# One mask product for a whole group of score tiles in place of one per tile

## What is computed

```
scores = jnp.einsum('bqd,bkd->bqk', hidden, keys)
scores = jnp.where(mask[:, None, :] == 0, NEG_INF, scores)
weights = jax.nn.softmax(scores, axis=2)
context = jnp.einsum('bqk,bkd->bqd', weights, values)
```

## Time and profile before

| | |
|---|---|
| median of 3 runs | 594.95 us (594.57 to 598.1) |
| span of the profiled execution | 602.9 us |
| TensorE busy | 565.9 us, 94% of the span |
| VectorE busy | 453.7 us, 75% |
| ScalarE busy | 377.1 us, 63% |
| mean granted TensorE clock | 0.997 of 2.4 GHz |

### The profile page before, as it was taken

One profiled execution on the slowest core, in us unless ns is written; L12 is line 12 of the kernel. 1 busy time (PEld: TensorE's weight loads), 2 busy tenths in 40 slices (PEclk: granted clock), 3 DMA queues, 4 the chain that ended last, 5 costly groups with the idle time before them and its releaser, 6 DMA issues.

```text
span 602.9 us, 12930 instructions
## 1 busy us (share of the span) xinstructions
PE 565.9 (94%) x3952; PEld 466.3 (77%) x3952; DVE 453.7 (75%) x1246; ACT 377.1 (63%) x729; POOL 257.7 (43%) x291
## 2 busy tenths in 40 slices
PE   7988999998989999999999999979889899999997
PEld 6787888886769999999999988867645555655654
DVE  5987888876645877778888863668888798867755
ACT  5676778864525777777777663345664684775643
POOL 4445665554550234455444445666635551310100
PEclk9999999999989999999999999999999999999999
DMA  8334654442238778879998827462112420200000
GB/s 237 107 108 148 210 196 163 145 167 88 106 123 254 278 255 268 276 230 285 273 274 276 274 85 285 138 213 79 52 37 73 130 96 36 71 2 35 36 36 35
DMA packets 47973, 93.15 MB, mean 154 GB/s; under 512 B 6990, under 2 KB 17306, under 8 KB 47778
## 3 DMA queue, kind: packets, MB, share of 16 engines
q1 hardware_dynamic: 39740, 74.34, 37.1%
q0 software_dynamic: 7440, 17.97, 9.9%
q10 hardware_dynamic: 726, 0.02, 0.1%
HBM read 61.32 MB, written 32.17 MB: 155 GB/s over the span
## 4 chain that ended last, share of the span: by engine, by line
PE 57%; DVE 20%; ACT 7%; issue 7%; POOL 4%; DMA 2%; SPq 2%; another core or an unknown queue 1%; ACTq 0%; DVEq 0%; POOLq 0%
PE bank L1336 12%; PE bank L1334 12%; PE bank L1335 11%; PE bank L1832 5%; DVE st L2408 3%; PE bank L1853 3%; PE bank L1854 2%; POOL yr L731 2%; DVE g3l L2485 2%; DVE xa L2399 2%; DVE sl L2480 2%; PE bank L1675 2%; PE bank L1320 2%; PE bank L1301 1%; DVE xa L2463 1%
## 5 line engine op out<-in xcount | busy, mean ns | idle before, releaser
L635 POOL DMA_INDIRECT rows_by_expert<-n,pos x64 | 64.6, 1009 | 53.6 <-DVE pos L2136 37.1
L683 POOL TENSOR_TENSOR yg<-yg,b 128x512 f32<-128x512 f32 x31 | 46.8, 1509 | 93.9 <-ACT yg L823 93.9
L731 POOL DMA_INDIRECT yr<-expert_out,out_row x64 | 65.0, 1016 | 33.4 <-issue 19.1
L1832 PE MATMUL bank<-m4Th,wint 128*128 128x512 f16 x192 | 69.0, 380 | 5.5 <-DVE sl L2480 3.3
L1334 PE MATMUL bank<-xTh,wph 128*128 128x256 f32 x248 | 72.3, 291 | 0.5 <-issue 0.4
L1336 PE MATMUL bank<-xTh,wpl 128*128 128x256 f32 x248 | 70.1, 283 | 0.0
L1335 PE MATMUL bank<-xTl,wph 128*128 128x256 f32 x248 | 70.1, 282 | 0.0
L1832 PE MATMUL bank<-m4Tl,wint 128*128 128x512 f16 x192 | 68.8, 379 | 0.0
L2301 DVE TENSOR_TENSOR wpl<-wraw,wph 128x1024 fp32r<-128x1024 f32 x40 | 49.0, 1224 | 11.3 <-ACT wph L823 11.2
L823 ACT ACTIVATE wph<-wraw 128x1024 fp32r<-128x1024 f32 x40 | 42.4, 1060 | 14.1 <-PE bank L1336 9.3
L2480 DVE SCALAR_TENSOR_TENSOR sl<-bank,sl 128x512 f32<-128x512 f32 x48 | 33.0, 688 | 22.5 <-ACT sl L1137 22.4
(11 more groups left out here) (352 smaller groups left out, 1740.6 us busy)
## 6 DMA issues: line engine op xcount, KB each, us to landing
wraw<-in_wexp SPq DMA_DIRECT2D x40, 512.0 KB
xg<-rows_by_expert SPq DMA_DIRECT2D x31, 256.0 KB, 4.1
expert_out<-yg SPq DMA_DIRECT2D x31, 256.0 KB, 3.5
x_shared<-x SPq DMA_DIRECT2D x8, 512.0 KB
xa<-x_shared SPq DMA_DIRECT2D x4, 1024.0 KB
out<-ost SPq DMA_DIRECT2D x8, 512.0 KB, 2.7
xin<-in_x SPq DMA_DIRECT2D x7, 512.0 KB, 4.2
stage<-in_wexp SPq DMA_DIRECT2D x8, 256.0 KB
```

The lines of the kernel that those rows point to most:

```text
L635: pool.indirect_dma_start(out=xs, out_offset=bass.IndirectOffsetOnAxis(ap=pos[p][:, k, j:j + 1], axis=0), in_=n2[p][:, j, :], in_offset=No ...
L683: pool.tensor_tensor(yg[u % 3], yg[u % 3], b2[:, bass.ds(e, 1), :].broadcast_to([P, 2, D]), ALU.add)\
L731: pool.indirect_dma_start(out=yr[:, c, k, j, :], out_offset=None, in_=ys, in_offset=bass.IndirectOffsetOnAxis(ap=out_row[:, b * GB + c, k, ...
L1832: last = mm(bank[:, 2 * (m % 2) + w, :], wt[:, k, m * P:(m + 1) * P], part[c][:, k, :], start=(q == 0 and k == 0), stop=(q == 1 and k == K ...
```

## The change

In `scores`, the mask product is taken out of the loop over the four tiles. Behind the loop stands one product of the same `onesb` by `barred`, whose 77 columns are read four times over (a broadcast operand), and which writes the 77 columns of each of the four tiles: 308 columns in all. It gives `s_done`. In `scores_half` the same is done for two tiles, 154 columns, and the wait for `mask_ready` moves from between the first tile and its mask to behind both tiles. The flag that begins an accumulation is now set on the first product of the bank alone, and not on the first of each tile.

```diff
@@ scores(g, b)
                 for j in range(GT):
                     o = bank[:, 6, j * P:j * P + KV]
                     for k in range(KD):
-                        mm(o, n1T[:, k, j * P:(j + 1) * P], ctxC[:, k, b, :], start=(k == 0), stop=False)
-                    last = mm(o, onesb, barred[:, b, :], start=False, stop=True)
-                last.then_inc(sem("s_done"), 1)
+                        mm(o, n1T[:, k, j * P:(j + 1) * P], ctxC[:, k, b, :], start=(j == 0 and k == 0), stop=(j == 0 and k == KD - 1),
+                           skip_group_check=(j > 0))
+                every = bank[:, 6, :].rearrange("p (j n) -> p j n", j=GT)[:, :, 0:KV]
+                mm(every, onesb, barred[:, b, :].unsqueeze(1).broadcast_to([P, GT, KV]), start=False, stop=True,
+                   skip_group_check=True)\
+                    .then_inc(sem("s_done"), 1)
@@ scores_half(h)
                 for j in range(2):
                     o, t = bank[:, 6 - 4 * h, j * P:j * P + KV], 2 * h + j
                     for k in range(KD):
-                        mm(o, n1T[:, k, t * P:(t + 1) * P], ctxC[:, k, 0, :], start=(k == 0), stop=False)
-                    if h == 0 and j == 0:
-                        pe.wait_ge(sem("mask_ready"), 1)
-                    last = mm(o, onesb, barred[:, 0, :], start=False, stop=True)
-                last.then_inc(sem("s_done"), 1)
+                        mm(o, n1T[:, k, t * P:(t + 1) * P], ctxC[:, k, 0, :], start=(j == 0 and k == 0), stop=(j == 0 and k == KD - 1),
+                           skip_group_check=(j > 0))
+                if h == 0:
+                    pe.wait_ge(sem("mask_ready"), 1)
+                both = bank[:, 6 - 4 * h, 0:2 * P].rearrange("p (j n) -> p j n", j=2)[:, :, 0:KV]
+                mm(both, onesb, barred[:, 0, :].unsqueeze(1).broadcast_to([P, 2, KV]), start=False, stop=True,
+                   skip_group_check=True)\
+                    .then_inc(sem("s_done"), 1)
```

## The result

The changed kernel takes 597.43 us, the median of 20 runs (594.54 to 603.62). The kernel before, on the same chip, takes 594.87 us, also 20 runs (593.42 to 598.2). The ratio is 1.004, with a 95% interval of 1.0024 to 1.0056: **slower by 0.4%**. That lies outside the predicted range, which ended at 596.8, and it is a loss where a gain of 0.4 us was forecast. It did stay within 1%, which had the chance of 0.95.

The account below looks back on a forecast made before the run. TensorE, busy 94% of the span, was taken to bound the kernel. Per full group -3 x 0.065 + 0.095 = -0.10 us, over four groups on the chain 0.40 us, gave 594.95 - 0.40 = 594.5 us, range 593.2 to 596.8.

Parts of the forecast that it names:

- The price of a tile: Scores loop on TensorE: a tile without mask takes 0.448 us in place of 0.513, so a removed product is worth 0.065.
- The wide product: Behind the four tiles of scores: 308 columns cost 0.13 us, 0.095 more than the narrow product.
- Rival 3: Scores: broadcast operand and four-piece target make the wide product dear, 595.4 to 595.8 us; chance 0.06.
- The sum per group: Scores of a full group: three removed products against the wide one's growth, -0.10 us, ends -0.35 and +0.09.
- The flags at nothing: Scores: removing the flag that begins an accumulation from three tiles of a group costs nothing.
- Rival 2: Scores: a removed product is worth its load and columns, 0.178 us, giving 593.2 us, or 591.9 with seven groups; chance 0.03.
- Which groups lie on the chain: First stage: four full groups' scores, at 73.29, 91.43, 109.45 and 128.42 us, lie on the chain of waits, gaining 0.40 us.
- What follows the four groups keeps its distance: After the scores: routing, counts and the first expert weight load depend on this stage, so 0.40 us carries to the end.
- rival 5: Whole kernel: the change isn't what it says; instruction order shows 23 products gone and nothing else moved, so given nothing.
- Rival 1: Ahead of the scores: the gain only lengthens TensorE's 3.1 us of idle time there, leaving 594.95 us; chance 0.15.
- Rival 4: TensorE's clock falls beside idle stretches: one more stretch gives 596.3 us, chance 0.10; four give 601.7 us, chance 0.03.
- The prediction's own test: Changed profile: the prediction is wrong if time moves over 2 us without a second fallen clock stretch besides that near 175 us.

Follow-up runs that it names:

- e6: Kernel before, with the four narrow mask products moved behind all four tiles in the seven full groups, instruction count kept: 594.92 us, ratio 0.9986.
- e8: Wide product in the seven full groups, with one product of 204 unread columns ahead of it, against the kernel before: 596.14 us, ratio 1.0017.
- e5: Kernel before with only the accumulation flags of the change, order and products as before: 595.83 us, ratio 0.9999.
- e7: Wide product in the seven full groups, three one-column products ahead of it, halves as before, against the kernel before: 595.11 us, ratio 0.9996.
- e9: The whole change measured again on another chip, against the kernel before: 597.38 us, ratio 1.0028.
- e10: The change plus 23 one-column products in TensorE's idle stretch at the start, against the kernel before: 594.43 us, ratio 0.9989.
- e12: The change plus a one-column product for each removed mask product, ahead of the wide one, against the kernel before: 595.5 us, ratio 1.0000.
- e18: The change plus 23 one-column products in the idle stretch at the start, a second time, against the kernel before: 605.84 us, ratio 1.0005.
- e11: Kernel before, scores untouched, its first 14 fillers as single 512-column passes, 28 instructions fewer: 596.74 us, ratio 1.0025.

## Why the prediction was wrong, step by step

**The price of a tile** was right: 0.45 us forecast for a tile without mask, 0.46 measured, and e6 to e8 show the same. Its reason was half right. I took 0.065 us as what a removed product is worth. It is what a mask *between float32 products* costs (0.06 measured: a quarter of what the 2.08 us have over four tiles of 0.46). Behind them a narrow one costs 0.14 / 4 = 0.035 us, so the gain was to be had with all four products kept.

**The wide product**: 0.13 forecast, 0.14 measured. Rival 3 (it is dear) is out; e7 has it without a loss.

**The sum per group**: -0.10 forecast, 2.08 - 1.98 = 0.10 measured. The flags at nothing: right (e5). Rival 2, where the Trainium skill's page "TensorE: Matmul & The Clock Gate" (Part 3, the section on the mechanism) would have made removed loads dear, is out too: the four loads of a tile are 0.19 us each (before, where no stretch of low clock falls into them), 0.76 in all, and the tiles are 0.46 us apart, so loads still hide. The same section of the Trainium skill also lets a load run ahead into a background weight buffer, so the rule was taken more narrowly than it stands there.

**Which groups lie on the chain**: wrong for this execution. The chain of the changed kernel passes through the scores at 19.06, 41.85, 60.89 and 133.25 us, four of them, but in the middle of the stage through GpSimd's scatters. So the chain's choice among nearly equal paths was taken for a fixed list. This mattered little in size.

**"What follows the four groups keeps its distance ... so the 0.40 us should carry to the end"**: this is the step that failed. It counted 23 products removed as time, and as nothing else. The order of instructions was indeed unchanged (rival 5 was rightly given nothing), but every later instruction of TensorE stood up to 46 places nearer to the start of the code. The distance that was not kept is that of code pieces to transfers. In the trace of before a piece starts 4.71 us ahead of the last store of zeros, which lands after 1.70 us; in the changed kernel's it starts 0.92 us behind it, and the store lands after 3.61. With the 0.4 us forecast and not gained, the miss is 2.0 + 0.4 = 2.4 us by e9 and 2.9 by the first measurement. The row that would have warned me, the instruction queue of the page, was not read, since its share is 0.4%.

**Rival 1** (gain absorbed): not the case at the scores, whose idle time fell from 3.1 to 2.8 us. With the number restored the ratios are 0.9986 to 1.0005; a gain of 0.4 us is 0.9993, and no ratio here tells it from none. At equal clock, by the estimate above, e6 and e7 lie 0.8 and 0.9 us below before, each within 0.7, but e10, e12 and e18 show no clear gain.

**Rival 4** (the clock) had the sign and about half the size, 596.3 us, but it isn't the main cause. Stretches at 1.2 GHz come and go between the runs of either kernel, and at equal clock the change is still 2 us slower in e9; of the first measurement it may be a part. The prediction's own test, "wrong if the time moved by more than 2 us without a second such stretch", can't be put to the profiled execution, which has stretches of its own (13.65 us from 13.15 us on, 3.41 us from 43.87). e9's profiled execution has none, and e9 moved by 2.0 us.

## What to carry to other kernels

In a kernel as tight as this one, a change in the *number* of an engine's instructions is a change of its own, apart from what they do. Before a gain or a loss of 0.2 to 0.4% is put down to an edit, run the edit with the number restored (products of one column in an idle stretch) and the old kernel with the number changed; here the two controls together pointed to the number at once. And read what the issuing engine waits for just ahead of a new stage, in every trace: one wait of 0.2 or of 1.8 us at line 491 told the traces apart, where sums over the first stage did not. And where a small product of another type stands between large ones, moving it behind them can be worth as much as merging it.

## What the runs showed of the hardware that I had not expected

- A store of zeros landed 1.7 to 2.0 us after its issue in twelve traces, and 3.6 to 3.8 us after it in the seven in which a 16 KB piece of TensorE's code started 0.9 to 1.7 us behind it.
- TensorE's code came in 33 pieces of 16 KB over the run, each 0.9 to 1.8 us long, and where one started 0.8 to 3.6 us behind a scatter the scatter's last packet ended after 3.96 us in place of 3.21.
- 28 instructions fewer at the start of a kernel of 12,930, by fillers of another kind and about the same time, made it 0.25% slower (e11, interval 0.07 to 0.43%).
- A bfloat16 product of 308 columns with a broadcast operand and a target in four pieces took 0.14 us to the next one, exactly as long as four products of 77 columns in a row.
- The same kernel took 595 to 596 us on the chips of the result and of e5 to e12 and 605 to 606 us on those of the others, more than anything that was changed here.
